# Folding the final weight of a mixture-of-experts block into the experts' second weights, and weighing results where they are made

## What is computed

```python
gating = softmax(X @ Wg + bg)                       # X: 4096 tokens x 256, 8 experts
top_k_indices = argsort(gating)[..., -2:]
h = silu((X @ W1 + b1) * (X @ W3 + b3))             # per expert, 256 -> 512
expert_outputs = h @ W2 + b2                        # per expert, 512 -> 256
topk_out = take_along_axis(expert_outputs, top_k_indices[..., None], axis=2)
topk_w = take_along_axis(gating, top_k_indices, axis=-1)
mixed = sum(topk_w[..., None] * topk_out, axis=2)
return mixed @ Wf + bf                              # then layernorm(x + this)
```

## Time and profile before

| what | us |
|---|---|
| median of 3 runs | 1925.81 |
| lowest and highest | 1922.15, 1928.32 |
| the profiled execution, own time | 1924.49 |
| its span from first to last instruction | 1922.8 |
| TensorE busy in the span | 1736.4 (90%) |
| VectorE, ScalarE, GpSimd busy | 1244.2, 898.1, 332.6 |

### The profile page before, as it was taken

The page is one execution under the profiler, slowest core; times in us unless marked ns, Lnnn a source line. Parts: engine busy times, 40 slices in busy tenths (PEclk is TensorE's granted clock), DMA queues, the critical chain, the costliest instruction groups (busy, mean ns, idle before and its releaser), DMA issues.

```text
span 1922.8 us, 28296 instructions
## 1 busy us (share of the span) xinstructions
PE 1736.4 (90%) x9130; PEld 910.4 (47%) x9131; DVE 1244.2 (65%) x2992; ACT 898.1 (47%) x1043; POOL 332.6 (17%) x468
## 2 busy tenths in 40 slices
PE   6999779999999999999999999977639999999965
PEld 3544334444444444444444444336516666666644
DVE  3688777777777777777777777326435555555536
ACT  2876754555555555555555554644402222222236
POOL 0000011021111211211112112114561111111111
PEclk9999889999999999899999999987659999999988
DMA  3464436020020110200201103036421111111144
GB/s 105 156 238 174 166 128 224 2 98 15 29 78 7 64 44 7 100 13 25 82 8 65 47 2 128 7 107 218 169 77 43 49 44 44 44 47 47 44 134 153
DMA packets 99595, 155.32 MB, mean 81 GB/s; under 512 B 10880, under 2 KB 60832, under 8 KB 99104
## 3 DMA queue, kind: packets, MB, share of 16 engines
q1 hardware_dynamic: 85088, 122.57, 19.4%
q0 software_dynamic: 14400, 31.37, 4.6%
HBM read 87.90 MB, written 65.35 MB: 80 GB/s over the span
## 4 chain that ended last, share of the span: by engine, by line
PE 69%; issue 7%; ACT 5%; DVE 4%; DMA 2%; SPq 1%; POOL 1%; ACTq 0%; POOLq 0%; DVEq 0%
PE att_ps_s L1017 23%; PE exp_ps_h L1649 13%; PE att_ps_o L1036 12%; PE att_ps_m L266 10%; PE exp_ps_y L1667 6%; ACT att_probs L1064 3%; PE exp_ps_t L1657 2%; DMA out_parts<-att_out_t 1%; PE exp_ps_x L1638 1%; DVE att_maxima L276 1%; POOL att_probs L1119 1%; DVE fin_stats L1180 1%; DVE fin_res L1870 0%; DVE fin_mixed L1863 0%; PE fin_ps_y L1221 0%
## 5 line engine op out<-in xcount | busy, mean ns | idle before, releaser
L1064 ACT ACTIVATE att_probs<-att_ps_s 128x1024 f32<-128x1024 f32 (+3 forms) x640 | 563.0, 895 | 461.8 <-PE att_ps_s L1017 454.3
L1017 PE MATMUL att_ps_s<-att_queries,att_keys 49*128 49x512 f32 (+3 forms) x2560 | 626.4, 557 | 17.8 <-ACT att_probs L1064 12.2
L276 DVE TENSOR_REDUCE att_maxima<-att_ps_m 128x1 f32<-128x512 f32 x768 | 487.4, 684 | 152.1 <-PE att_ps_m L266 147.5
L266 PE MATMUL att_ps_m<-att_keys,att_queries 48*128 48x512 f32 (+3 forms) x1280 | 493.6, 591 | 20.4 <-DVE att_maxima L279 14.7
L266 PEld LDWEIGHTS att_ps_m<-att_keys,att_queries 48*128 48x128 f32 x1280 | 190.5, 187 | 323.6 <-DVE att_maxima L276 149.9
L1017 PEld LDWEIGHTS att_ps_s<-att_queries,att_keys 49*128 49x128 f32 x2560 | 241.1, 189 | 125.1 <-ACT att_probs L1064 87.9
L279 DVE CUSTOM_DVE_ANT_0 att_ps_m<-att_ps_m,att_future 128x128 f32<-128x128 f32 (+3 forms) x512 | 240.5, 514 | 69.6 <-PE att_ps_m L266 68.3
L1036 PE MATMUL att_ps_o<-att_probs,att_values 128*32 128x512 f32 (+3 forms) x2560 | 273.3, 543 | 12.1 <-POOL att_probs L1119 12.1
L1649 PE MATMUL exp_ps_h<-keep_w,exp_rows_t 128*128 x568 | 261.8, 604 | 5.2 <-DVE exp_rows_t L1683 5.2
L1725 ACT ACTIVATE exp_hidden<-exp_product 128x512 f32<-128x512 f32 x71 | 44.9, 632 | 347.5 <-DVE exp_product L1708 347.5
L1119 POOL TENSOR_SCALAR_AFFINE_SELECT att_probs<-att_probs 128x512 f32<-128x512 f32 x128 | 81.1, 634 | 480.2 <-ACT att_probs L1064 480.1
(11 more groups left out here) (179 smaller groups left out, 1426.3 us busy)
## 6 DMA issues: line engine op xcount, KB each, us to landing
att_queries<-q_parts SPq DMA_DIRECT2D x64, 192.0 KB
att_keys<-k_parts SPq DMA_DIRECT2D x64, 192.0 KB
exp_rows<-sorted_rows SPq DMA_DIRECT2D x71, 129.0 KB, 2.3
v_rows<-pre_v_sb SPq DMA_DIRECT2D x8, 1024.0 KB, 4.8
q_parts<-pre_waves SPq DMA_DIRECT2D x16, 512.0 KB, 5.7
k_parts<-pre_waves SPq DMA_DIRECT2D x16, 512.0 KB, 6.3
att_values<-v_rows SPq DMA_DIRECT2D x32, 256.0 KB
out_parts<-att_out_t POOLq DMA_DIRECT2D x32, 256.0 KB, 6.1
```

Source lines behind the costliest of these rows:

```text
L266: pe.matmul(bank[:, 0:width], self.queries[g % 2][half, c, r, P * q:P * q + P], self.keys[g % 2][half, k, r, 0:width], start=True, stop=Tr ...
L276: dve.tensor_reduce(to, bank[:, 0:width], AX.X, ALU.max).then_inc(self.s_mr, 1)
L1017: mm = pe.matmul(score_tile(unit, first, last)[:, e], keys[g % 2][half, k // TPC, r, P * (k % TPC):P * (k % TPC) + P].bitcast(F32), querie ...
L1064: act.activation(probs[:, step % PROBS, DUO * r:DUO * r + DUO, first:last], score_tile(unit, first, last), ACT.Exp, scale=SCALE).then_inc( ...
```

## The change

1. **Fold.** In `route`, W2 of every expert is replaced by W2 @ Wf and b2 by b2 @ Wf, in place. This is done in ten blocks of four experts: two of bias2 (first), eight of w2. For each, TensorE turns the block (`turn_weight`, 8 transposes into ps_n), ScalarE copies it to `turned` (`keep_turned`), TensorE multiplies by wf (`multiply_weight`, into a new single ps_f) and ScalarE copies the product back (`keep_folded`). Four folds start in rounds 7 to 10 of the list (`FIRST_FOLD`, `FOLDS_AMONG`), six follow behind the last round.
2. **Loads.** SyncE orders Wf in round 2, behind a wait for all attention results, blocks of W2 in rounds 1 to 4 and half of bias1 in round 5. The other half shares its place with `turned`; ScalarE orders it after its last fold copy.
3. **Weighing.** Each sorted row also carries its two gate weights (260 numbers for 258) and the number of its result row. VectorE works out the gate of a row in `find_places` (one more operation), and ScalarE multiplies the result by it (`weigh`, lag 3, last in its list) before the store. The two results of a token lie next to each other in expert_rows.
4. **End.** `finish` loads each chunk in one transfer of 1 MB (2 KB runs), four chunks ahead, the first in two halves. TensorE adds the two results by multiplying with the identity into ps_y (four buffers). VectorE, ScalarE and GpSimd do the residual, norm and store as before, with deeper buffers, no loops, the list order residual (lag 0), scale_and_shift (lag 1), and the last store in two halves.
5. **Waits.** The experts wait for the folds only at the first projection out, and for bias1 only at the first `multiply`.

```diff
-ROW, TOKEN, FIRST_EXPERT = D + 2, D, D + 1
+ROW, FIRST_ROW, FIRST_EXPERT, FIRST_WEIGHT, SECOND_WEIGHT = D + 4, D, D + 1, D + 2, D + 3
+FOLDS_AMONG, FIRST_FOLD = 4, 7
...
@@ route, SyncE
-                while i >= 1 and len(later) > loads * (NCH - 1 - i) // (NCH - 1):
-                    sp.dma_start(*later.pop(0)).then_inc(s_last, 16)
+                if i == 2:
+                    for j in range(2):
+                        sp.wait_ge(attended.s_store[j], 32 * CHUNKS // 2)
+                        sp.wait_ge(attended.s_kept[j], 16 * CHUNKS // 2)
+                    sp.dma_start(wf[:, :], Wf.rearrange("(k p) n -> p k n", p=P)).then_inc(s_wf, 16)
+                if 1 <= i <= HK:
+                    to, rows = weight_blocks(w2, W2)[i - 1]
+                    sp.dma_start(to, rows).then_inc(s_w2[i - 1], 16)
+                if i == HK + 1:
+                    sp.dma_start(flat(bias1[:, TPC:NE]), flat_rows(b1[TPC:NE]).partition_broadcast(P)).then_inc(s_b1, 16)
...
@@ route, TensorE
+                if i + 2 > FIRST_FOLD:
+                    pe.wait_ge(s_ft, min(i + 2 - FIRST_FOLD, FOLDS_AMONG))
                 turn_rows(pe, ps_n, x1[:, i * TPC:i * TPC + TPC, 0:D], ident[:, :]).then_inc(s_np, 1)
...
+            def turn_weight(j, p):
+                rows, loaded, count = folds[j]
+                pe.wait_ge(loaded, count)
+                pe.wait_ge(s_nt, min(j + FIRST_FOLD - 1, NCH))
+                if j >= 1:
+                    pe.wait_ge(s_ft, j)
+                turn_rows(pe, ps_n, rows, ident[:, :]).then_inc(s_fp, 1)
+
+            def multiply_weight(j, p):
+                if j == 0:
+                    pe.wait_ge(s_wf, 16)
+                pe.wait_ge(s_ft, j + 1)
+                if j >= 1:
+                    pe.wait_ge(s_folded, j)
+                multiply_rows(pe, ps_f, turned[:, p], wf).then_inc(s_fm, 1)
...
-            pipelined(pe, NCH, [(project, 1), (turn_x1, 2), (count_before, 3), (project_gates, 2)])
+            pipelined(pe, NCH, [(project, 1), (among(multiply_weight), FIRST_FOLD + 1), (turn_x1, 2), (count_before, 3), (project_gates, 2),
+                                (among(turn_weight), FIRST_FOLD)], unrolled=True)
+            pipelined(pe, len(folds) - FOLDS_AMONG,
+                      [(lambda j, p: turn_weight(j + FOLDS_AMONG, (j + FOLDS_AMONG) % 2), 0),
+                       (lambda j, p: multiply_weight(j + FOLDS_AMONG, (j + FOLDS_AMONG) % 2), 1)], unrolled=True)
...
@@ route, ScalarE
+            def keep_turned(j, p):
+                act.wait_ge(s_fp, j + 1)
+                if j >= 2:
+                    act.wait_ge(s_fm, j - 1)
+                act.copy(turned[:, p], ps_n[:, :]).then_inc(s_ft, 1)
+
+            def keep_folded(j, p):
+                act.wait_ge(s_fm, j + 1)
+                act.copy(folds[j][0], ps_f[:, :]).then_inc(s_folded, 1)
...
-                (exponential, 2)])
+                (exponential, 2),
+                (among(keep_turned), FIRST_FOLD),
+                (among(keep_folded), FIRST_FOLD + 1)], unrolled=True)
...
+            act.wait_ge(s_fm, len(folds))
+            act.dma_start(flat(bias1[:, 0:TPC]), flat_rows(b1[0:TPC]).partition_broadcast(P)).then_inc(s_b1, 16)
...
@@ experts
-            pe.wait_ge(routed.s_last, routed.last_loads)
...
+                if not since(s, 1):
+                    pe.wait_ge(routed.s_folded, routed.folds)
...
+                dve.scalar_tensor_tensor(gate[:, mine], rows[:, p, FIRST_WEIGHT:FIRST_WEIGHT + 1], is_first[:, mine],
+                                         rows[:, p, SECOND_WEIGHT:SECOND_WEIGHT + 1], ALU.mult, ALU.max).then_inc(s_gate, 1)
...
+                if not since(s, 1):
+                    dve.wait_ge(routed.s_b1, 32)
...
+            def weigh(s, p):
+                act.wait_ge(s_r, s + 1)
+                act.wait_ge(s_gate, s + 1)
+                act.activation(result[:, p], result[:, p], ACT.Copy, scale=gate[:, p:p + 1]).then_inc(s_gated, 1)
+            pipelined(act, SLOT_TILES, [(activate, 1), (keep_hidden, 2), (weigh, 3)], body=4)
...
@@ finish
+            sp.dma_start(picked[:, 0, 0:half], rows_in[0][:, 0:half]).then_inc(s_begin, 16)
+            sp.dma_start(picked[:, 0, half:TPC], rows_in[0][:, half:TPC]).then_inc(s_pick[0], 16)
+            for i in range(1, NCH):
+                if i >= 4:
+                    sp.wait_ge(s_y, (i - 3) * TPC)
+                sp.dma_start(picked[:, i % 4], rows_in[i]).then_inc(s_pick[i % 4], 16)
...
+                    for r in range(TOPK):
+                        mm = pe.matmul(ps_y[i % 4][:, t], ident[:, :], picked[:, i % 4, t, r], start=(r == 0), stop=(r == TOPK - 1))
+                    mm.then_inc(s_y, 1)
...
-            pipelined(dve, NCH, [(mix, 0), (scale_and_shift, 3), (residual, 2)])
+            pipelined(dve, NCH, [(residual, 0), (scale_and_shift, 1)], unrolled=True)
```

245 lines of the change are left out of this document (117 added, 128 removed).

## The result

The changed kernel takes 1937.89 us (median of 6 runs, 1931.67 to 1940.34), the kernel before 1924.37 beside it (1919.14 to 1928.32): ratio 1.0067, 95% interval 1.0045 to 1.009. Repeated on another occasion it was 1.0055 (1.0035 to 1.0075). So it is slower by 0.6%, 11 to 13 us. (One of the ten executions of the repetition, 2893.65 us at a granted clock of 0.555, is not in that ratio.) My likeliest case was no change (1928.9). What came is the case "slower than 1931.6", which I had given 0.35; the time lies inside the range of 1917 to 1942, just above rival C at half its price (1936). The profiled run took 1940.34, its span 1938.6.

A forecast was written before the change was run, and what follows sets the result against it. It took the folds' end, with the experts' TensorE work queued behind it, as the bound instead of the stores, and VectorE as the end's pace: +19.3 - 16.2 = +3.1 us on 1924.49, 1927.6, median 1928.9, range 1917 to 1942.

The forecast's parts named there:

- rival C: Folds and experts' start: gaps keep TensorE's clock at half; 1944 us in full, 1936 at half its price; chance 0.17.
- Part 1, E: Routing's folds: E, when TensorE ends the last fold, at 1444; 1436.5 at full clock, 1457 with half clock to multiplication 4.
- no longer the bound: GpSimd's stores at the routing's end: last lands near 1420, pads near 1422, both before the last fold's end.
- Part 2, start: Experts' start: third projection 16.5 us after the last fold, at 1460.5 for 1441.23: +19.3 us, bounds +10.5 and +34.
- Part 3, steps: Experts' steps stay at 5.82 us despite added VectorE and ScalarE operations; only +0.5 us at the end.
- rival E: Experts: the added ScalarE step lengthens each expert step, up to 1960 us; chance 0.03.
- Part 4, end: End after the experts: weighing, transposes, one copy per chunk and Wf's load gone: -16.2 us, bounds -19 and -12.5.
- Head: Start of the end stage: first half chunk lands at 1857.2, residual 0 at 1864.2 for 1871.34: -7.1 us.
- Pace: End stage, VectorE's chunks: 3.7 us each, seven in 25.9 us for 34.3: -8.4 us.
- Tail: Last store in halves, 256 KB less behind the last instruction: -0.7 us.
- Rival D: End stage bound by transfers, not VectorE: 1933 us; chance 0.07.
- Rival B: Folds run at full clock throughout, bias lands early, end starts warm: -7 us, 1919; chance 0.23.

The follow-up runs named there:

- second trace: The changed kernel, unedited, run once more beside other kernels: ratio 1.0055 (1.0035 to 1.0075).
- filled kernel: Changed kernel plus dummy multiplications, four ahead of multiplications 1 to 3 and two ahead of the last two gates: ratio 1.0069.
- lines broken: Changed kernel with the first bias half loaded in round 6, GpSimd also awaiting each four stores' landing in the last three rounds: ratio 1.0012.
- bias early: Changed kernel with the turned block moved, so SyncE loads the first bias half in round 6, ahead of the folds: ratio 1.0038.
- one store: Changed kernel with the last rows' store whole instead of in two halves: 55.1 us from last result store to span's end.
- spread folds: Changed kernel with eight folds in rounds 3 to 10: ratio 1.0032; with GpSimd also awaiting each four stores from the third round's rows: 1.0008.

## Why the prediction was right and wrong

**Part 1, E.** Forecast 1444, measured 1458.9 and 1457.2, past my own sign of being wrong (1452) and even past the walk with half clock up to multiplication 4 (1457). This is the step that failed: I walked the folds with durations and one semaphore delay each, and took every signal of TensorE to come at the end of its work. (a) Projection 7 ended at 1377.0, and 1378.0 in the second trace, for 1372.0 in my walk, before any multiplication had been done; in the other kernels with the first fold in round 7 it ends between 1367.6 and 1374.5. That is 5 us that I can't assign; runs differ by as much there. (b) From there to E I had 72.0 us and it was 81.9 and 79.2. In the first trace multiplication 1 begins 3.9 us later than in the walk, 3.3 of it the first lag; multiplications 1 to 3, taken at 5.3 us each, took 6.6: +3.8; from multiplication 2 to 3 it is 7.2 us for 4.2, +3.1, with the lag of 3.9 in it; a fold behind the rounds took 4.88 us for my 4.6: five spacings, +1.4. Against that, the gates of round 7 and the turn behind them took 7.0 us for 9.3: -2.3. The sum is 9.9. The lags were not in the walk. No wait in the trace of before shows one of more than 1.7 us, but its semaphore updates, on which the walk did not draw, show the counts 3.6 to 5.6 us late. The filled kernel shows that the clock term doesn't come off by itself: with two multiplications at 3.6 the lag before the next one grew from 3.9 to 9.4 and E came no earlier. With the lines broken, the lag before multiplication 3 goes, and with it that multiplication's slow clock; the distance from the end of projection 7 to E is then 75.0, near my 72.0.

**The stores.** I wrote that they are "no longer the bound" and costed them at nothing, naming E as their cover. Their landing was covered: it came at 1428.8, not near 1420, as the counts of the last round were late too, but E was 1458.9. What I didn't ask is what their issue does to the engines that work beside them. So the stores were still in the chain, not through their data, but through TensorE's late signals.

**Part 2, start.** Projection 2 at E + 14.9, forecast E + 16.5. The bias half was ordered at 1458.96 and used at 1463.92: 4.96 us, for my 5.9. The Trainium skill's formula ("DMA: Bandwidth & Descriptors", section on the anatomy of one DMA), which that section gives for transfers issued by GpSimd, made 4.4 us of it as an estimate; the measured time is nearer to that than to mine. Projection 1 took 5.39, between the two bounds. With the bias early the start is E + 12.4: the cost of ScalarE's late order is 2.5 us, not the 6 that a wait for a landing suggests, since the first projection lies under it.

**Part 3, steps.** The step stayed at 5.82 us (last result store 33.26 later for a third projection 32.59 later, the 0.67 being the weighing of the last result). Right, with 0.5 forecast, and rival E, a longer step, is refuted.

**Part 4, end.** Forecast -16.2, which has part 3's 0.5 in it; measured -17.4 behind the last result store, and with the 0.67 ahead of it -16.8. Head: residual 0 came 12.3 us after this store, for 21.1 before, -8.8, with the 0.67 -8.1 for my -7.1; the first half chunk landed 3.9 us after its order, as forecast, but residual 0 followed in 5.8 us, where I had 7.0 at half clock. Pace: 24.6 us for seven chunks (3.53 each at the end) for my 25.9, against 34.3: -9.7 for -8.4. Tail: from residual 7 to the end of the span 18.2 us for 17.1 before, +1.1 for my -0.7, and 18.3 with one store: the halves bring nothing. The three last stores issue 0.98 us apart, so the last half waits for GpSimd. That the parts add up to within 0.6 us of the forecast is in part luck: head and pace gained 2.3 us more than I had, and the tail lost 1.8. Rival D, the end bound by transfers, is refuted: there is one chunk each 3.53 us, and TensorE doesn't wait for rows behind the first.

**Sum.** On the profiled runs I forecast 1927.6, and it was 1940.3: +12.7, of which +13.3 is the third projection and -0.6 the end. That this lies inside my range is owed to the width that rival C had given it, not to the walk. Rival C had the right place and, at half its price (1936), nearly the right time, but for the most part the wrong reason: it put the loss down to the clock, which is 3.8 of the 9.9 us behind projection 7. Rival B's clock came true for two multiplications of the filled kernel and brought nothing there.

**Left open.** What inside the chip makes TensorE's signals late during an unbroken line of indirect stores isn't settled: the records' ends of TensorE are modelled, so it may be its work or only its signals. Nor is it shown why the amount of its work since the line's start matters. Not tried: the spread folds with pauses in the early rounds only, which might beat the kernel before, as E is at 1425.3 there and the stores of the last two rounds would be done earlier; the pauses in the changed kernel without any other edit; and the pauses in the kernel before.

## What to carry to other kernels

Work moved into an engine's idle time is not free if that time is spent waiting for a chain through other engines; walk the chain with every instruction that runs beside it, and ask of each long line of DMA issues who else must signal in that time. When results of an engine are seen late without a reason in the profile, compare its semaphore updates with its records, and try to break the line of stores beside them with a wait for their landing. And price the parts alone: here the end gained all it promised, and the folds lost more.

## What was not expected of the hardware

- While GpSimd issues indirect stores without a pause (one each 1.27 us), TensorE's signals can come late. Beside lines of eight they were on time with up to 20 multiplications since the line's start, and 0.5 to 5.9 us late with 25 or more, in the kernel before too. Beside lines of 16 and more waits of 9, 12 and 22 us were seen, and beside lines of four with a wait for the landing between them waits up to 1.2 us.
- Holding such stores back until they form one long line beside TensorE's work makes it worse (distance 94.3 us for 84.6); holding them until that work is over doesn't (79.5).
- SyncE's eight pad writes took 12.1 to 18.0 us beside unbroken lines in eleven traces, 9.4 in the one where TensorE was idle beside them, and 8.1 and 8.2 beside broken ones. Why is not shown.
- A 1 MB broadcast load ordered by ScalarE onto an otherwise quiet queue was usable 4.96 us after its issue.
